# Transposing weights and normalised tokens by DMA in place of TensorE, in a fused autocorrelation-attention and FFN kernel

## The reference

```
corr = ifft(fft(q) * conj(fft(k)))            # over the 64 positions
w, idx = top_k(corr, 8);  w = softmax(w)      # per batch, head, channel
out[i] = sum_t w_t * v[min(idx_t + i, 63)]
x = x + tanh(g_xattn) * out
h = silu(layernorm(x) @ W_gate.T) * (layernorm(x) @ W_up.T)   # 512 -> 1792, f16 weights
x = x + tanh(g_ffn) * (h @ W_down.T)                          # 1792 -> 512
```

## Time and profile before

| what | value |
|---|---|
| median of 3 runs | 243.51 us (242.82 to 243.72) |
| the profiled execution, its own time | 243.05 us |
| its span | 241.2 us |
| mean granted TensorE clock | 0.965 |
| PE busy | 216.8 us, 90% of the span |
| DVE, POOL, ACT busy | 161.8, 122.4, 102.4 us |

### The profile page before, as it was taken

One profiled execution on the slowest core, in us unless ns is written; L12 is line 12 of the kernel. 1 busy time (PEld: TensorE's weight loads), 2 busy tenths in 40 slices (PEclk: granted clock), 3 DMA queues, 4 the chain that ended last, 5 costly groups with the idle time before them and its releaser, 6 DMA issues.

```text
span 241.2 us, 6322 instructions
## 1 busy us (share of the span) xinstructions
PE 216.8 (90%) x2608; PEld 149.7 (62%) x2608; DVE 161.8 (67%) x437; ACT 102.4 (42%) x197; POOL 122.4 (51%) x136
## 2 busy tenths in 40 slices
...
DMA packets 4507, 12.61 MB, mean 52 GB/s; under 512 B 640, under 2 KB 1024, under 8 KB 4096
## 3 DMA queue, kind: packets, MB, share of 16 engines
...
...
## 4 chain that ended last, share of the span: by engine, by line
PE 84%; DVE 10%; POOL 2%; DMA 1%; issue 1%; ACT 1%; POOLq 0%
PE psum L634 42%; PE psum L747 20%; PE psum L625 11%; PE psum L711 6%; PE psum L719 2%; DMA x_sb<-x 1%; PE psum L685 1%; DVE probs L540 1%; DVE xn L592 1%; DVE probs L556 1%; DVE raw_stats L497 1%; PE psum L671 1%; DVE prod L522 1%; POOL rstd L374 1%; PE psum L673 1%
## 5 line engine op out<-in xcount | busy, mean ns | idle before, releaser
L634 PE MATMUL psum<-xt_hi,wg 128*128 128x128 f16 x448 | 54.6, 221 | 0.6 <-DVE xt_lo L596 0.6
L634 PE MATMUL psum<-xt_lo,wg 128*128 128x128 f16 x448 | 54.3, 221 | 0.0
L634 PE MATMUL psum<-xt_hi,wu 128*128 128x128 f16 x448 | 53.5, 219 | 0.0
L634 PE MATMUL psum<-xt_lo,wu 128*128 128x128 f16 x448 | 53.5, 219 | 0.0
L634 PEld LDWEIGHTS psum<-xt_hi,wg 128*128 128x128 f16 x448 | 43.7, 99 | 9.9 <-issue 8.4
L409 POOL TENSOR_TENSOR hid_lo<-hid,hid_hi 128x512 f16<-128x512 f32 (+1 forms) x32 | 33.4, 1046 | 30.4 <-ACT hid_hi L491 30.4
L634 PEld LDWEIGHTS psum<-xt_hi,wu 128*128 128x128 f16 x448 | 43.7, 98 | 3.0 <-issue 2.5
L402 POOL TENSOR_TENSOR mixed_lo<-mixed,mixed_hi 128x512 f16<-128x512 f32 x30 | 35.0, 1175 | 18.9 <-ACT mixed_hi L474 18.7
L634 PEld LDWEIGHTS psum<-xt_lo,wg 128*128 128x128 f16 x448 | 44.3, 99 | 0.1
L634 PEld LDWEIGHTS psum<-xt_lo,wu 128*128 128x128 f16 x448 | 43.8, 98 | 0.5
L747 PE MATMUL psum<-wd,hid_hi 128*128 128x512 f16 x112 | 42.5, 380 | 0.0
...
## 6 DMA issues: line engine op xcount, KB each, us to landing
out<-x_sb SPq DMA_DIRECT2D x8, 256.0 KB, 2.0
...
ctx_sb<-ctx SPq DMA_DIRECT2D x1, 1024.0 KB, 20.4
...
x_sb<-x SPq DMA_DIRECT2D x2, 256.0 KB, 3.9
ctx_sb<-ctx SPq DMA_DIRECT2D x1, 512.0 KB, 6.1
```

The lines of the kernel that those rows point to most:

```text
L634: last = nc.tensor.matmul(psum[:, bank, a * P:(a + 1) * P], w[:, k, m * P:(m + 1) * P], xt[:, e, k, :], start=(k == 0 and part == 0), stop ...
```

## The change

For pairs 1 to 7 (`BY_DMA`) the weights and the normalised tokens are split into f16 parts while their rows still lie as they were computed, and each f16 part is transposed from SBUF to SBUF by a DMA that SP issues (`transpose=True`). Pair 0 keeps the f32 transposes on PE.

- `wt`, `w_hi`, `w_lo` of a pair become `w_rows_hi` (ACT), `w_rows_lo` (POOL) and `w_t` in two parts (SP, one DMA each for high and low); `wspec` waits for both DMAs.
- `xt`, `x_hi`, `x_lo` become `x_rows_hi` (ACT), `x_rows_lo` (POOL) and `x_t` in two parts (SP); `gate` waits for both DMAs.
- The low parts were DVE's, from PSUM; they are now POOL's, from SBUF. `xn` has one buffer in place of two.
- SP walks through the list too, with `store` steps of its own.
- The code can also take whole f32 products for pairs named in `WHOLE`. All its entries are empty, so that no product is changed, but its f32 table (`consts32`, 704 columns) is loaded, in two pieces and ahead of pair 1's inputs. The f16 table comes in one piece after these, and `kspec:0` waits for all of it. The first piece of ctx goes through SP's queue.
- The list `ORDER` is new from its first line to its last.

```diff
@@ settings
+WHOLE = {"k": (), "q": (), "p": (), "w": (), "m": ()}
+BY_DMA = (1, 2, 3, 4, 5, 6, 7)
@@ sync
             load(x_sb, xv, 0, 1, x_loaded[0])
-            sp.dma_start(consts[:, 0:FIRST], table[:, 0:FIRST]).then_inc(first_loaded, 16)
+            sp.dma_start(consts32[:, 0:WHOLE_FIRST], table32[:, 0:WHOLE_FIRST]).then_inc(whole_first, 16)
+            load(ctx_sb, cv, 0, 1, ctx_loaded[0])
+            sp.dma_start(consts32[:, WHOLE_FIRST:WHOLE_CONSTS], table32[:, WHOLE_FIRST:WHOLE_CONSTS])\
+              .then_inc(whole_loaded, 16)
             load(x_sb, xv, 1, 2, x_loaded[1])
             load(ctx_sb, cv, 1, 2, ctx_loaded[1])
-            sp.dma_start(consts[:, FIRST:CONSTS], table[:, FIRST:CONSTS]).then_inc(forward_loaded, 16)
+            sp.dma_start(consts[:, :], table).then_inc(consts_loaded, 16)
...
+            for step, p, n in order:
+                e = p % 2
+                if step == "w_t":
+                    if n == 0:
+                        sp.wait_ge(w_rows_high, nth("w_rows_hi", p))
+                        if p >= 2:
+                            sp.wait_ge(w_spectra, 2 * (p - 1))
+                    else:
+                        sp.wait_ge(*split_count("w_rows_lo", p, 0))
+                    to, rows_of = ((w_hi, w_hi_rows), (w_lo, w_lo_rows))[n]
+                    sp.dma_start(to[:, e, :].rearrange("p (c r) -> p c r", r=P), rows_of[:, e, :], transpose=True)\
+                      .then_inc(w_moved[n][e], 16)
+                if step == "x_t":
...
+                    to, rows_of = ((xt_hi, xn_hi), (xt_lo, xn_lo))[n]
+                    sp.dma_start(to[:, e, :, :], rows_of[:, e, :], transpose=True).then_inc(x_moved[n][e], 16)
+                if step == "store":
@@ gpsimd
+                if step == "x_rows_lo" and mine:
+                    pool.wait_ge(x_rows_high, nth("x_rows_hi", p))
+                    if p >= 2 and by_dma(p - 2):
+                        pool.wait_ge(x_moved[1][e], nth_moved(p - 2))
+                    nc.gpsimd.tensor_tensor(xn_lo[:, e, :], xn[:, :], xn_hi[:, e, :],
+                                            ALU.subtract).then_inc(split_sems["x_rows_lo", False], 1)
@@ tensor
                 if step == "gate":
                     if n == 0:
-                        pe.wait_ge(xt_low, p + 1)
+                        if by_dma(p):
+                            for part in range(2):
+                                pe.wait_ge(x_moved[part][e], nth_moved(p))
+                        else:
+                            pe.wait_ge(xt_low, nth("x_lo", p))
@@ list, from xt:0 to gate:0
-xn:0 prod:2 xt:0 wt:1 prod:2.1 x_hi:0 p_hi:2 x_lo:0 w_hi:1 p_lo:2
-stats1:3 gate:0
+rstd2:0 prod:2.1 p_hi:2 xn:0 p_hi:2.1 p_lo:2 q_norm:3 xt:0 p_lo:2.1 x_hi:0 stats1:4 wspec:1 q_hi:3 x_lo:0
+rstd1:4 lags:2 mix_prod:1 gate:0
```

More of the change, by code:

```diff
@@ L97 @@
 ORDER = """
[L98 to L147, removed]
@@ L148 @@
-silu:7 gate:7.1 hid:7 h_hi:7 h_lo:7 up:7.1 tanh:7.1 silu:7.1 gate:7.2 hid:7.1 up:7.2 tanh:7.2 h_hi:7.1
-silu:7.2 h_lo:7.1 gate:7.3 hid:7.2 up:7.3 tanh:7.3 h_hi:7.2 silu:7.3 down:7 hid:7.3 h_lo:7.2 h_hi:7.3 h_lo:7.3
-down:7.1 down:7.2 down:7.3 out:7
+stats1:0 rstd1:0 k_hi:0 k_lo:0 q_norm:0 stats1:1 q_hi:0 k_hi:1 q_lo:0 rstd1:1 kspec:0 k_lo:1 q_norm:1 qspec:0
+kcopy:0 kspec:1 kcopy:0.1 prod:0 vspec:0 prod:0.1 p_hi:0 p_hi:0.1 p_lo:0 stats1:2 vcopy:0 kcopy:1 lags:0
+p_lo:0.1 kcopy:1.1 max:0 vcopy:0.1 vspec:1 q_hi:1 match:0 lags:0.1 vcopy:1 q_lo:1 vcopy:1.1 max:0.1 exp:0
@@ new lines @@
+rstd1:2 qspec:1 match:0.1 prod:1 prod:1.1 p_hi:1 sum:0 p_hi:1.1 p_lo:1 q_norm:2 exp:0.1 p_lo:1.1 sum:0.1
+q_hi:2 scale:0 lags:1 scale:0.1 wt:0 max:1 w_hi:0 gates:0 w_lo:0 k_hi:2 match:1 wspec:0 k_lo:2 q_lo:2
+mix_prod:0 exp:1 kspec:2 mix_prod:0.1 wspec:0.1 m_hi:0 sum:1 kcopy:2 m_hi:0.1 mix_prod:0.2 scale:1 mix:0
+mix_prod:0.3 m_hi:0.2 m_lo:0 m_lo:0.1 m_hi:0.3 w_rows_hi:1 mix:0.1 scales:0 m_lo:0.3 m_lo:0.2 kcopy:2.1 w_t:1
+vspec:2 stats1:3 w_rows_lo:1 mix:0.2 vcopy:2 residual:0 vcopy:2.1 rstd1:3 k_hi:3 qspec:2 w_t:1.1 prod:2
@@ new lines @@
+rstd2:0 prod:2.1 p_hi:2 xn:0 p_hi:2.1 p_lo:2 q_norm:3 xt:0 p_lo:2.1 x_hi:0 stats1:4 wspec:1 q_hi:3 x_lo:0
+rstd1:4 lags:2 mix_prod:1 gate:0 q_lo:3 max:2 m_hi:1 m_lo:1 mix_prod:1.1 up:0 match:2 m_hi:1.1 k_lo:3 tanh:0
+k_hi:4 gate:0.1 k_lo:4 silu:0 exp:2 m_lo:1.1 wspec:1.1 sum:2 kspec:3 mix_prod:1.2 scale:2 up:0.1 kcopy:3 hid:0
+kcopy:3.1 mix_prod:1.3 tanh:0.1 vspec:3 m_hi:1.2 silu:0.1 w_rows_hi:2 m_lo:1.2 q_norm:4 gate:0.2 m_hi:1.3
+w_t:2 hid:0.1 vcopy:3 m_lo:1.3 vcopy:3.1 mix:1 h_hi:0 mix:1.1 w_rows_lo:2 mix:1.2 tanh:0.2 qspec:3 residual:1
@@ new lines @@
+k_hi:5 h_lo:0 w_t:2.1 up:0.2 h_hi:0.1 prod:3 rstd2:1 silu:0.2 p_hi:3 gate:0.3 h_lo:0.1 prod:3.1 up:0.3
+tanh:0.3 hid:0.2 p_lo:3 p_hi:3.1 xn:1 wspec:2 p_lo:3.1 down:0 silu:0.3 x_rows_hi:1 hid:0.3 h_hi:0.2 x_t:1
+mix_prod:2 h_lo:0.2 m_hi:2 lags:3 h_hi:0.3 down:0.1 q_hi:4 x_rows_lo:1 max:3 h_lo:0.3 mix_prod:2.1 x_t:1.1
+down:0.2 match:3 m_lo:2 m_hi:2.1 q_lo:4 down:0.3 wspec:2.1 m_lo:2.1 exp:3 kspec:4 mix_prod:2.2 gate:1 sum:3
+m_hi:2.2 kcopy:4 m_lo:2.2 mix_prod:2.3 kcopy:4.1 up:1 tanh:1 scale:3 m_hi:2.3 silu:1 m_lo:2.3 stats1:5
@@ new lines @@
+w_rows_hi:3 vspec:4 w_t:3 hid:1 mix:2 k_lo:5 vcopy:4 mix:2.1 out:0 vcopy:4.1 mix:2.2 store:0 w_rows_lo:3
+h_hi:1 qspec:4 gate:1.1 prod:4 rstd1:5 w_t:3.1 residual:2 up:1.1 tanh:1.1 rstd2:2 p_hi:4 silu:1.1 prod:4.1
+p_lo:4 gate:1.2 hid:1.1 p_hi:4.1 xn:2 h_hi:1.1 p_lo:4.1 wspec:3 tanh:1.2 h_lo:1 x_rows_hi:2 up:1.2 mix_prod:3
+x_t:2 mix_prod:3.1 m_hi:3 h_lo:1.1 silu:1.2 m_hi:3.1 lags:4 m_lo:3 hid:1.2 gate:1.3 max:4 h_hi:1.2 up:1.3
+tanh:1.3 h_lo:1.2 stats1:6 down:1 x_rows_lo:2 silu:1.3 match:4 m_lo:3.1 down:1.1 x_t:2.1 hid:1.3 wspec:3.1
```

275 lines of the change are left out of this document (221 added, 54 removed).

## The result

The changed kernel took **235.08 us** (median of 4 runs, 234.52 to 235.86) against 243.16 for the kernel before beside it (4 runs, 242.19 to 243.72). The ratio is 0.967, 95% interval 0.963 to 0.972. A second measurement gave 234.24 us and 0.964 (0.962 to 0.967). The forecast was 238.2 us with a range down to 235.3. The sign was right and the gain too small by a third: 3.3% came where 2.2% was forecast.

The account below looks back on a forecast made before the run. PE was taken to bound the packed piece from `gate:0`, a chain through DVE, ACT and POOL the start. 243.05 - 5.8 - 1.5 + 3.0 - 0.95 = 237.8, plus 0.46 for the median: 238.2 us, range 235.3 to 243.0 (its own 235.3 to 240.5).

Parts of the forecast that it names:

- The three pieces: Kernel before: start to `gate:0` 41.5 us, a piece packed with PE work 196.5 us, a tail of 3.2 us.
- the start: Up to `gate:0`: later f16 table and new list delay `gate:0` from 41.51 to 44.5 us, +3.0 us.
- -5.8 - 1.5 ... - 0.95: Packed piece: 13 transposes gone -5.8 us, `wspec:1` and `lags:2` moved ahead -1.5, slow first `gate:0` matmuls avoided -0.95.
- my 0.45: Packed piece: typical PE time in us for one step of four f32 transposes, 13 of them making -5.8 us.
- the clock at `gate:0`: First 32 matmuls of `gate:0`: `wspec:1` and `lags:2` take the slow stretch instead, 2.84 to 1.89 us, -0.95 us.
- The sum's own bounds: Whole kernel: transposing step at 0.4 to 0.6 us, start +1 to +4.5 us; 234.3 to 240.4 us without stalls.
- The walk: Start: new list followed with durations from the rows, `residual:0` at 36.7 us where it came at 34.96.
- The room at pair 1: From `x_rows_lo:1` ending at 66.0 to PE reaching `gate:1` at 71.0: 5.0 us, so a 3.5 us DMA fits.
- the slower rival: `gate` and `wspec` of pairs 1 to 7: PE waits for late DMAs, 254 us if landing takes 7.0; chance 0.13.
- The two rules of the Trainium skill: DMA transposes: one page gives 1309 ns a block against 390 on TensorE, estimate 265 us; another ordinary DMA speed, 238.
- POOL and DVE: Packed piece, a rival: POOL or DVE bind now and then, 0.5 us for each of 7 pairs, 241.7 us; chance 0.13.
- The start ate: Start, a rival: table another 2 us late and the walk 2 us worse eat the gain, 242 to 243 us; chance 0.08.

Follow-up runs that it names:

- The three experiments: The runs e3_scatter, e11_before_grouped and e9_best, which change how often PE visits 64-row or 64-column products: 240.60, 241.17 and 234.89 us.
- e3_scatter: The changed kernel with 17 more PE visits to 64-row or 64-column products, same work in all: 240.60 us, ratio 0.991.
- e11_before_grouped: The kernel before, with the three parts of mix put together for pairs 2 and 4 to 7, taking out 6 of 37 visits: 241.17 us, ratio 0.993.
- e9_best: The changed kernel with the loads of before and q_norm:2, lags:1, vspec:3 and qspec:7 moved in the list, two visits fewer: 234.89 us, ratio 0.965.
- the first placement: The kernel before, old list and loads, each PE transposing step of pairs 1 to 7 replaced in its place by row splits and DMAs: 249.78 us, ratio 1.031.
- the second: The kernel before, its PE sequence and loads kept, with row splits and DMA transposes written directly behind scale and xn: 248.74 us, ratio 1.021.

## Why the prediction fell short

**The three pieces** were right, and so was that PE sets the middle one alone. Span before less span after is 7.8 us, and the packed piece and the start give it to 0.1.

**Which step failed.** The sum took from the packed piece only what is removed or moved out of it: "-5.8 - 1.5 ... - 0.95". It gave every step of PE one price wherever it stands, and so held the new sequence itself for free. It isn't. The piece lost 11.4 us where 8.25 was worked out:

- 6.4 for the 13 transposing steps (I had 5.8). The step is 0.50 with going in and out, my 0.45 left that out. 0.6 of the miss.
- 1.55 for `wspec:1` and `lags:2` (0.75 and 0.80; I had 1.5).
- 0.8 for the clock at `gate:0`, the first 32 (I had 0.95).
- the rest, 2.6, for 14 visits fewer (I had nothing), 0.19 each. This is the miss. The three experiments give 0.19, 0.27 and 0.16 a visit.

The visit is a rough unit. PE's products here have three shapes: full, on 64 rows (spectra) and into 64 columns (mix). From the last pair of mix at 57.8 us to the spectrum behind it at 58.13 it is 0.31 us too, inside one visit. By changes between the three shapes the starts count 81 before, 52 after, 81 in `e3_scatter`, 67 in `e11_before_grouped`, 49 in `e9_best`, and with waits and the first 32 left out one change costs 0.11, 0.12 and 0.10 us in the three experiments, nearer to one another than the prices of a visit. The change has 29 fewer: 3.0 us or 0.10 each, the 2.6 above and some 0.4 that lie in the prices of the steps that left. No run has the new list with all transposes on PE, so that the 2.6 are this remainder and not a measurement by themselves.

A sign of it was in the rows: 32 matmuls that follow a spectrum stand there at 1.89, which is 59 ns each where their starts lie 56 ns apart. The prediction took 1.8 for such a step and left the 0.09 out. And the diff shows the whole list as new; the prediction looked in it for waits, not for what stands beside what on PE. The sum's own bounds reached down to 234.3 us, which holds the 235.08; the stated range stopped at 235.3. And the start, 0.65 us longer than forecast, hid a part of the miss by luck.

**The start.** +3.0 forecast, +3.65 in the profiled execution, and +2.4 to +4.0 in the other executions that are the same up to `gate:0`. The f16 table came at 9.3 where I had 8.5: it was issued at 3.53 and took 5.8 us for 352 KB. The walk gave `residual:0` at 36.7, it was 38.08 (36.2 to 38.4 in the others). What `gate:0` waited behind in the profile was `lags:2`, released by POOL's two differences; the prediction had `lags:2` running straight on from `wspec:1` and `x_lo:0` ending last. The chain of the kernel after:

```profile
40.43 0.64 ACT prod_hi L539
41.07 0.07 issue
41.14 2.64 POOL prod_lo L473 x2
43.77 0.14 issue
43.91 0.21 PE psum L836
```

That the late table would cost the start 1 us of its own is not borne out (the loads of before changed nothing that can be told from noise).

**The DMAs.** I took 2 to 3.5 us, it is 2.5 in the median, SP's 1.19 included, with 7 of the 28 between 3.5 and 4.3. The room at pair 1 was predicted as 5.0: POOL's `x_rows_lo:1` ended at 66.97 (66.0 forecast) and `gate:1` began at 71.57 (71.0), 4.6 us. At `wspec:2` it was 58.04 to 62.57, 4.5 us (4.4). Their parts had landed at 69.42 and 60.50, so 2.1 us are left at each. That a landing of 5.4 us is where the slower rival begins fits: 5.2 in the median cost 0.5 to 1.3 us (235.58 against 235.08 and 234.24), no more than the scatter, 8.2 cost about 20, where that rival's arithmetic gives (8.2 - 4.7) x 7 = 24.5.

**The two rules of the Trainium skill.** The trace agrees with the Trainium skill's section on the X-bar transpose ("Advanced Engine Details and Errata") roughly: 128 KB transposed land after 2.5 us, a plain store of twice the bytes after 2.3; the issue isn't as fast, 1.19 against 0.43 us. The table of the Trainium skill's "VectorE: DVE Perf Modes", section on the three transpose paths, 1309 ns for a block by DMA against 390 on TensorE, does not add up block by block: four blocks here take 2.5 us to land, where an estimate from that page has 5.2. And where PE is the bound, the DMAs idle and the list is written for them, the slower path is the better one.

**The rivals.** A late DMA did not happen in this list. In the old one it cost PE 6.4 us of waits in the first placement (249.8 us in all); in the second (248.7) PE waited on the other queues instead. POOL and DVE didn't bind, even with 14 differences moved between them. The start ate 3.65 us, not all.
